# Six transformer layers on one core: the loop body opens with the transposes of the attention output, and ScalarE makes the diagonals

## The reference

```python
for i in range(DEPTH):          # 6
    x = attn_layer(shift_tokens(x), Wqkv[i], q_scale[i], k_scale[i], Wo[i]) + x
    x = ffn_layer(shift_tokens(x), ln_g[i], ln_b[i], W1[i], b1[i], W2[i], b2[i]) + x
```

## Time and profile before

| what | value |
|---|---|
| median of 3 runs | 2667.56 us (2662.51 to 2668.82) |
| the profiled execution, its own time | 2666.3 us |
| its span, first to last instruction | 2664.3 us |
| PE busy in the span | 2264.3 us (85%) |
| DVE, ACT, POOL busy | 1827.0, 1360.7, 1220.4 us |
| mean granted TensorE clock | 0.907 |

### The profile page before, as it was taken

The page is one execution under the profiler, slowest core; times in us unless marked ns, Lnnn a source line. Parts: engine busy times, 40 slices in busy tenths (PEclk is TensorE's granted clock), DMA queues, the critical chain, the costliest instruction groups (busy, mean ns, idle before and its releaser), DMA issues.

```text
span 2664.3 us, 85876 instructions
## 1 busy us (share of the span) xinstructions
PE 2264.3 (85%) x34185; PEld 1699.2 (64%) x34185; DVE 1827.0 (69%) x3373; ACT 1360.7 (51%) x2449; POOL 1220.4 (46%) x1450
## 2 busy tenths in 40 slices
PE   5878885289998999989999889999799998999994
PEld 3555453266776677767777676767576776677673
DVE  5444543767777777777777777777777777777764
ACT  3444443155564556554655455655455564556551
POOL 3333342255454545454545544554545454545440
PEclk7565656599998999999999999999999999999997
DMA  1000000100000000000000001000010000000000
GB/s 53 11 13 16 21 15 28 54 2 2 0 0 2 8 33 0 0 0 8 33 0 0 0 0 40 0 0 0 0 38 3 0 0 0 8 9 0 0 1 16
DMA packets 15696, 27.50 MB, mean 10 GB/s; under 512 B 5731, under 2 KB 11278, under 8 KB 14862
## 3 DMA queue, kind: packets, MB, share of 16 engines
q1 hardware_dynamic: 13566, 25.56, 2.9%
q10 hardware_dynamic: 2064, 1.05, 0.1%
HBM read 21.22 MB, written 5.37 MB: 10 GB/s over the span
## 4 chain that ended last, share of the span: by engine, by line
PE 49%; DVE 15%; issue 10%; ACT 5%; POOL 1%; DVEq 1%; ACTq 0%; DMA 0%; SPq 0%; POOLq 0%
PE scb L1212 7%; PE tb L1256 6%; PE wide L1232 6%; DVE nrm L1008 4%; PE wide L1201 4%; PE rawb L1174 4%; PE scb L1219 3%; PE rawb L1176 3%; PE rawb L1175 3%; PE tb L1292 2%; PE tb L1286 2%; PE tb L1287 2%; PE scb L1208 2%; DVE dg L1055 2%; PE tb L1248 2%
## 5 line engine op out<-in xcount | busy, mean ns | idle before, releaser
L808 POOL TENSOR_TENSOR part<-cs 128x256 f32<-128x256 f32 x384 | 278.5, 725 | 838.6 <-DVE cs L1004 835.9
L1004 DVE TENSOR_TENSOR cs<-rawb,rots 128x1024 f32<-128x1024 f32 x384 | 469.5, 1223 | 104.0 <-ACT sq L847 92.4
L817 POOL TENSOR_TENSOR part<-part,nrm 128x512 f32<-128x512 f32 x384 | 396.9, 1065 | 156.3 <-DVE nrm L102 149.3
L847 ACT ACTIVATE sq<-rawb 128x512 f32<-128x512 f32 x384 | 229.2, 597 | 451.2 <-PE rawb L1176 446.2
L863 ACT ACTIVATE V<-wide 128x512 f32<-128x512 f32 x384 | 230.1, 599 | 122.3 <-PE wide L1192 107.0
L809 POOL TENSOR_TENSOR part<-cs 128x256 f32<-128x256 f32 x384 | 279.7, 728 | 0.0
L1029 DVE TENSOR_REDUCE mx<-scb 128x8 f32<-128x512 f32 x192 | 132.3, 689 | 206.6 <-PE scb L1212 206.6
L300 POOL TENSOR_SCALAR g_th<-g_th,g_scal 128x512 f32<-128x512 f32 x64 | 141.3, 2208 | 241.5 <-ACT g_th L350 241.5
L1232 PEld LDWEIGHTS wide<-V,pT 64*32 64x32 f32 x12288 | 185.1, 107 | 89.7 <-issue 89.7
L1232 PE MATMUL wide<-V,pT 64*32 64x65 f32 x12288 | 215.1, 219 | 24.6 <-issue 24.3
L1008 DVE TENSOR_REDUCE nrm<-sq 128x16 f32<-128x1024 f32 x192 | 232.0, 1209 | 0.0
(11 more groups left out here) (208 smaller groups left out, 4687.9 us busy)
## 6 DMA issues: line engine op xcount, KB each, us to landing
stage<-w_qkv_dram SPq DMA_DIRECT2D x6, 1536.0 KB, 6.8
scratch<-g_osb SPq DMA_DIRECT2D x8, 512.0 KB, 2.6
wo<-w_o_dram SPq DMA_DIRECT2D x6, 512.0 KB, 3.5
w<-w_dram SPq DMA_DIRECT2D x6, 384.0 KB, 3.0
g_oden<-inverses SPq DMA_DIRECT2D x128, 8.0 KB
w<-w_dram SPq DMA_DIRECT2D x6, 192.0 KB, 2.9
g_oc<-scratch SPq DMA_DIRECT2D x32, 32.0 KB
out_dram<-x ACTq DMA_DIRECT2D x1, 1024.0 KB, 5.1
```

The costliest lines, as they stand in the source:

```text
L808: nc.gpsimd.tensor_tensor(dst[:, :, 0, :], c[:, :, 0, :], s[:, :, 1, :], ALU.add)
L817: nc.gpsimd.tensor_tensor(p3, p3, nrm[:, 2, UH * u:UH * u + UH].unsqueeze(2).to_broadcast([P, UH, HD]), ALU.mult).then_inc(scaled, 1)
L847: nc.scalar.activation(sq[:, u % RING, :], rawb[:, u % 2, :], ACT.Square).then_inc(squared, 1)
L1004: nc.vector.tensor_tensor(dst, src, tab, ALU.mult).then_inc(turned, 1)
```

## The change

Four things move, and no computation is added or removed.

1. PE's body opens with the four transposes of O, the raw units 0 and 1 between and behind them, and `project_out`; only then `spread_root`, and the transposes 0 to 3 of Q and K in a row, and the first scores. Raw unit 2 moves up to a place behind transpose 4.
2. POOL does `prepare` first in its body, and the eight `apply_norms` after it.
3. `diagonals` moves from DVE to ACT, behind `square(n, 1)`; DVE's body opens with two rotations, and `add_attention` comes right after them, `norm_x` after that.
4. `means` and `variances` change halves of `tb`, and `variances` moves from ahead of `values` to a place behind its first two units.

Renamed variables (`u` to `i` in `values` and `copy_values`) change nothing, so V is laid out as it was.

```diff
@@ POOL @@
             def step(n, b, F, A, C, E):
-                if A:
-                    for u in range(NUN // 2):
-                        apply_norms(n - 1, u, F)
                 if F:
                     prepare(n, b)
                 if A:
-                    for u in range(NUN // 2, NUN):
+                    for u in range(NUN):
                         apply_norms(n - 1, u, F)
@@ ACT @@
+            def diagonals(r, n):
+                act.wait_ge(root_ready, n)
+                for i in range(TT):
+                    last = nc.scalar.activation(dg[:, i, :], idf[:], ACT.Copy, scale=nrm[:, 2, NORMS + i:NORMS + i + 1])
+                last.then_inc(dg_ready, 1)
...
+                if C:
+                    copy_oT(t, 0)
+                    copy_oT(t, 1)
+                if F:
+                    square(n, 0)
+                if C:
+                    copy_oT(t, 2)
+                    copy_oT(t, 3)
+                if F:
+                    square(n, 1)
+                if E:
+                    diagonals(r, n)
@@ DVE @@
-                if E:
-                    diagonals(r)
-                    norm_x(r)
-                if A:
-                    center(a, 0)
                 if F:
                     rotate(n, 0)
                     rotate(n, 1)
                     sum_squares(n, 0)
+                if C:
+                    add_attention(t, bt)
+                if E:
+                    norm_x(r)
                 if first is not None:
                     split(first, 2)
+                if A:
+                    center(a, 0)
...
@@ PE @@
                 if k == 0:
                     pe.wait_ge(o_read, (t + 1) * NG)
-                    pe.wait_ge(root_ready, t + 2)
+                    need(pe, dev_ready, t)
                 elif k == 1:
-                    need(pe, dev_ready, t)
-                    if E:
-                        pe.wait_ge(xn_ready, t)
+
+                    pe.wait_ge(v_step, (t + 1) * V_BODY + 1)
...
-                if j < 2:
+                if j == 0:
                     if C:
-                        pe.wait_ge(ot_copied, (r + 1) * NO + 3 + j)
-                else:
+                        pe.wait_ge(xf_ready, r + 2)
+                elif j == 2:
                     pe.wait_ge(hid_ready, UP + r * FC + 1)
...
+                if F:
+                    values(n, l, 0)
+                    values(n, l, 1)
                 if C:
-                    variances(t)
-                if F:
-                    for j in range(NV):
+                    variances(t, E)
+                if F:
+                    for j in range(2, NV):
                         values(n, l, j)
```

More of the change, by code:

```diff
@@ L916, in step @@
                 if F:
-                    square(n, 1)
+                    square(n, 2)
                 if A:
@@ L1050, in deviate @@
                 dve.wait_ge(mean_ready, t + 1)
-                nc.vector.tensor_tensor(dev[:], xf[:], tb[:, 0, 0:T], ALU.subtract).then_inc(dev_ready, 1)
-            def diagonals(r):
-                for i in range(TT):
-                    last = nc.vector.tensor_scalar(dg[:, i, :], idf[:], nrm[:, 2, NORMS + i:NORMS + i + 1], None, ALU.mult)
-                last.then_inc(dg_ready, 1)
+                nc.vector.tensor_tensor(dev[:], xf[:], tb[:, 1, 0:T], ALU.subtract).then_inc(dev_ready, 1)
             def norm_x(r):
@@ L1178, in values @@
             def values(n, l, j):
-                half, u = j // NU, j % NU
+                half, i = j // NU, j % NU
                 if j == 0:
@@ L1257, in project_out, with means, variances @@
                 last.then_inc(y_ready, 1)
[L1259 removed]
+            def means(t):
+                pe.wait_ge(xf_ready, t + 1)
+                mm(tb[:, 1, 0:T], mean1[:], xf[:], start=True, stop=True).then_inc(mean_ready, 1)
+            def variances(t, E):
                 if E:
                     pe.wait_ge(x_updated, B + t)
[L1262 to L1265 removed]
                 pe.wait_ge(dsq_ready, t + 1)
                 for i in range(TT):
[L1268 removed]
+                    last = mm(tb[:, 0, i:i + 1], dsq[:, P * i:P * i + P], mean1[:, 0:1], start=True, stop=True)
                 last.then_inc(var_ready, 1)
@@ L1297, in step @@
                 l = n // B
+                if C:
+                    transpose_o(t, 0, E)
+                    transpose_o(t, 1, E)
+                if F:
+                    raw(n, l, 0)
+                if C:
+                    transpose_o(t, 2, E)
+                    transpose_o(t, 3, E)
+                if F:
+                    raw(n, l, 1)
+                if C:
+                    project_out(t)
                 if E:
@@ L1364, in step @@
                 if C:
-                    means(t, E)
+                    means(t)
                 if A:
```

60 lines of the change are left out of this document (11 added, 49 removed).

## The result

The changed kernel takes 2789.81 us (median of four runs, 2781.13 to 2794.09), the kernel before 2668.19 us beside it. The ratio is 1.0448, with a 95% interval of 1.0424 to 1.0472: slower by 4.5%. The forecast was 2755 us, between 2705 and 2805. The direction and most of the size came as worked out; 34 us more came than forecast.

A forecast was written before the change was run, and what follows sets the result against it. PE's work and stalls bound each body: 2.88 us more in 40 plain bodies (+115.2), openings -32.8, ramp-up +5, together +87.4 on the span, giving 2755 us, range 2705 to 2805.

The forecast's parts named there:

- Raw 0 waits for the preparation: Body head: PE's raw unit 0 stalls for POOL's prepare, 1.9 us a body, bounds 1.5 and 2.2.
- `project_out` waits 0.3: Body head: the projection waits for the last copy of a transpose, 0.3 us, bounds 0 and 0.6.
- Third group 0.58, first scores 1.02: Body head: third Q/K transpose group waits 0.58 us for the first copy, first scores 1.02 for the fourth.
- Third weighing 1.02: Later in the body: without the projection as cover, the third transposed probabilities' use waits for their copy, +1.02 us.
- The end: +0.13: Body end: first values still waits for DVE's read of O; variances moved behind two values, net +0.13 us.
- The clock falls in every body: Rival, slower: low clock for 3 us of work behind raw 0's wait, about 1.5 us x 45, 2820 us; 4%.
- A gap of 1.9 us lies nearer to the second: Step against a clock fall: raw 0's gap resembles the plain body's 1.5 us at full clock, not the opening's 7.64.
- The term for the preparation beside the splits: Layer openings: POOL's preparation takes 3.86 us beside DVE's splits instead of 2.40, +1.46 us each.
- so DVE is in time: Layer openings: DVE can take up scores at about 20.6 us, PE starts them at 19.7; the 10.9 us excess goes.
- the opening keeps its gap: Rival, slower: at layer openings raw 0 or scores wait for DVE's splits, 5 x 10.9 stay, about 2810 us; 6%.
- DVE sets the pace: Rival, faster: the wait before values leads back through DVE's own work, so its relief shortens bodies, about 2545 us; 4%.
- the preparation costs nothing: Rival, no difference: raw unit 0 at the head is not held by prepare, 86 us less, 2669 us; 4%.

The follow-up runs named there:

- experiment 3: Changed kernel with project_out and add_attention back at their old places: 2819.91 us; the same with the diagonals also back on DVE: 2742.19 us.
- experiment 1: Changed kernel with the first two groups of O's transposes done three times over, filling PE's gap ahead of raw 0: 2773.84 us.
- experiment 4: Changed kernel with the diagonals back on DVE: 2787.16 us; kernel before with only the diagonals moved to ACT: 2649.94 us.
- the last experiment: Rebuilt version with O and Q/K transposes alternating (2583.28 us), further changed: raw 5, its rotation and square sum ahead of the projection, raw 7 earlier: 2527.89 us.

## Why the prediction was right, and where its sum was off

Step by step, with what the traces have:

1. *Raw 0 waits for the preparation: 1.9 us a body.* The mechanism is right, the size too small: 2.2 to 2.4 us, just past the bound of 2.2. The preparation lasted its 2.40 us. What failed is the way there and back: 0.39 us from PE's end to POOL where the sum had 0.3, and 0.38 from POOL's end to PE (1632.79 to 1633.17) where it had 0.1.
2. *`project_out` waits 0.3.* 0.42 at full clock, 0 in a body with a low clock. Right.
3. and 4. *Third group 0.58, first scores 1.02.* 0.58 and 1.00.
5. *Third weighing 1.02.* 1.02, and experiment 3 with the diagonals on DVE gives 0.9 back a body. What the prediction said of cover there, that the diagonals "would cost their 0.7" without the projection, was wrong: without it `spread_root` waited 1.26 us idle, since ACT has them behind the square of raw 1 and not only their own 0.68 us, and the clock made more of it, 78 us in all.
6. *The end: +0.13.* From the fourth weighing's start to the first `values` it was 3.46 us (1609.88 to 1613.34) and is 3.39 (1666.42 to 1669.81); from there to the O groups 6.64 us instead of some 6.5. Net +0.08.

A plain body at full clock came out at 45.30 us against 45.21, closer than item 1 alone would allow (+0.4): the old stalls were also larger than the 2.07 us I had counted. In the earlier trace rows the third Q and K group starts at 1581.03, 0.15 us behind the three groups from 1579.57 on (at 0.44 each), the next group 0.07 late, and `spread_root` took 0.55 us to the next start where it now takes 0.45. That is 0.3 us which the change removed and my sum left out. The two errors cancel, so that the 45.2 us came out this well is luck; in the body shown each stall by itself was right to 0.4 us.

The sum that failed is the one over bodies. Of the 33.8 us between the forecast's 87.4 and the 121.2 of plain bodies, openings and ramp:

- **The clock, 21 us.** "The clock falls in every body" had 4%, at about 1.5 us a body. It fell in 18 of 40 bodies, for 1.17 us. The step that failed is the comparison behind it: "A gap of 1.9 us lies nearer to the second", the plain body's 1.5 us that the clock had outlived, than to the 7.64. Between those two rows the trace of before had more, and I didn't look for it: at each opening `hidden(2)` waits 1.97 to 1.99 us for DVE, and behind two of these five waits the granted clock falls to 0.50, behind three it holds (rows in the last section). That is a fall in some of the cases at nearly the length forecast for raw 0, so the rival should have been priced as a term with a share of the bodies, and not as all or none. The section of the Trainium skill named beside it ("TensorE: Matmul & The Clock Gate", "Loop structure matters more than you think") says that a long wait inside the loop, there one for a DMA, can drop the clock each time round. This trace agrees in part: in 18 plain bodies and in all five openings, not in the other 22.
- **The openings, 9 us.** They lost 23.7 us and not 32.8: 48.5 us each against a forecast of 46.7. The term for the preparation beside the splits was right: raw 0's stall is 1.10 us longer than in a plain body, on a preparation 1.27 us longer (3.67 against 2.40), where the sum had 1.46. The step that failed is "so DVE is in time". Its sum left out DVE's third split, 2.4 us, which stands ahead of the first scores: DVE takes these up 0.8 us late, and the delay reaches PE as a wait of 0.66 us at `hidden(2)`. The kernel before had the same wait, 1.97 us long. The clock behind raw 0's wait, 1.18 us up to the projection, was not in the sum either (the prediction's signs had an opening "without a low clock", and all five had one), but it doesn't add to this: with the clock held (experiment 1) the openings were only 0.3 us shorter, and the wait at `hidden(2)` took up the rest. It is 1.56 us there from start to start, nearly all of the distance from the forecast's 46.7 us to the 48.3 of these bodies. The rival that the opening keeps its gap is refuted: nothing of the 7.64 us is left, and experiment 4 shows that the order closed it. By the rule of the Trainium skill on the port pair ("SBUF — State Buffer", "SBUF: two separate sides") the openings would have cost an estimated 10 us more. The trace agrees with it in part: the second of POOL's four instructions took 1.30 us beside DVE's splits and 0.40 in a plain body, which the rule would explain, but the third and fourth took 0.71 and 0.81 us where they take 0.63 and 0.72. In sum the preparation grew by 1.27 us a time and not by the 1.46 of the earlier trace rows and 2 more.
- **Plain bodies at full clock, 3.6 us**, 40 times 0.09.
- The ramp came to the forecast's sum (+5.1), though not as two bodies alike: the first got 0.65 us longer and the second 4.5, with a fall of the clock in it. The part outside the marks gave -0.7.

"DVE sets the pace" and "the preparation costs nothing" are refuted by the traces: DVE idled 5.77 us for the first square ahead of the first rotation of the full-clock body (6.01 in the longer one), and raw 0 waited in all 48 bodies. The first of the two was close to something, though. The wait ahead of `values` does lead back through DVE to raw 5, and what the last experiment did was to start that chain earlier. It gave 1.2 us a body; rotation 5 still waits 0.27 us for its square.

## What to carry to other kernels

A unit of work that sits between a producer and a consumer is cover, and moving it is charged twice: at the place it leaves and at the place where it now waits. Here the projection, moved to the head, exposed a copy of 1.02 us at the place it left, and the raw units, taken away from the head again, exposed waits of 0.36, 0.78 and 0.86 us. Interleaving two kinds of transposes, each covering the other's copy, left a wait of only 0.28 us ahead of the scores (0.60 in the last version).

Work that must wait for the last instruction of the previous iteration (here the preparation that overwrites `xh` and `xl`) doesn't belong at the head of the next one, as long as there is one buffer, whatever the order on its own engine. And where an engine waits for a chain on another, look for the idle time earlier in that chain: a rotation and a sum of squares went into 2.15 us of idle DVE, and this, together with the moves of raw 5 and raw 7, was worth 55 us.

When a change puts a wait of a new length in a loop, look through the whole trace for waits of that length, rare places included, and at the clock behind each. Count the clock as a term of its own with a range for the share of the iterations, and show it by filling the gap with idle work. Don't add a fall of the clock to a wait that comes behind it for another engine: the one can hide in the other, as at the openings here.

## What the runs showed of the hardware

Whether the granted clock falls behind a wait of some 2 us is not told by the length of that wait. Two layer openings of the kernel before, timeline of PE and windows just behind these places:

```profile
1200.33 0.70 PE L1286 MATMUL tb<-xn,w 128*128 128x256 f32 x2 [1.97 <-DVE hid L1066]
...
1550.27 0.70 PE L1286 MATMUL tb<-xn,w 128*128 128x256 f32 x2 [1.97 <-DVE hid L1066]
```

```profile
1202.00:1204.00 2.00, 2.00 (x59) 1.39 (x53) 1.38 (x3) 1.90 (x2) 1.29 (x2) 0.50 0.00 0
...
1551.00:1553.00 2.00, 2.00 (x88) 1.35 (x89) 1.67 (x4) 1.54 (x2) 1.18 (x2) 1.00 0.00 0
```

Behind 1.97 us of idle time the clock fell in the one and held in the other. In the changed kernel the idle time before raw 0 was 2.00 to 2.23 us in the 18 plain bodies in which the clock fell, and 1.91 to 2.23 us in the 22 in which it held. In experiment 3 with the diagonals on DVE the same place had 1.91 to 2.27 us, and the clock fell in 2 of 40. What tips it was not found; filling the wait (experiment 1) ended it, and with a second wait of 1.26 us behind it (experiment 3) it fell in 28 of 40.

Two diagonals of 128 x 128 take ScalarE 0.68 us together, where its copies of four times their width take 1.09 for two: the duration doesn't go by the width alone.
